# Banded attention and a routed expert layer on one core: the last batch routed in two groups instead of computed densely, ids loaded unchecked, projection writes earlier, score banks by kind

## The reference, cut to what matters

```python
x = _layernorm(x + attention(x))       # 16 heads of 16, key within 64 of the query or before:
                                       # mask = max(causal, window), softmax, out projection
x = _layernorm(x + moe(x))
# moe: 16 experts, top 4 of 16 inside the best 2 of 4 groups, weights normalised, times 2.5
scores = sigmoid(x @ router_weight.T); sc = scores + e_bias
group_scores = sum of the top 2 of each group of 4; keep 2 groups; tidx = top_k(masked, 4)
tw = scores[tidx] / (sum + 1e-20) * 2.5
g = x @ gate_w[e].T; u = x @ up_w[e].T; y = (silu(g) * u) @ down_w[e].T   # 256 -> 128 -> 256
routed = sum over the 4 chosen of tw * y;  shared = the same MLP, width 256, for every token
return routed + shared
```

## Time and profile before

| | us |
|---|---|
| median of 3 runs | 1260.3 (1251.3 to 1264.51) |
| profiled execution | 1256.9, its span 1254.9 |
| PE busy | 1056.3 (84%) |
| DVE busy | 863.1 (69%) |
| ACT busy | 626.5 (50%) |
| POOL busy | 469.5 (37%) |
| granted clock of TensorE, mean | 0.941 |

### The profile page before, as it was taken

One profiled execution on the slowest core, in us unless ns is written; L12 is line 12 of the kernel. 1 busy time (PEld: TensorE's weight loads), 2 busy tenths in 40 slices (PEclk: granted clock), 3 DMA queues, 4 the chain that ended last, 5 costly groups with the idle time before them and its releaser, 6 DMA issues.

```text
span 1254.9 us, 24541 instructions
## 1 busy us (share of the span) xinstructions
PE 1056.3 (84%) x8451; PEld 590.1 (47%) x8451; DVE 863.1 (69%) x1833; ACT 626.5 (50%) x1409; POOL 469.5 (37%) x682
## 2 busy tenths in 40 slices
PE   7696999989777998988997779888898776998895
PEld 4353333344422555544554445454555445654463
DVE  6486787777884666788667676687567556587453
ACT  4323677766444555654555456554455463322332
POOL 7552111152156102223444633214625630286332
PEclk9897999999897999999999899999999898998998
DMA  5753257420123433234366634232636643443320
GB/s 177 214 173 109 69 198 267 125 68 26 49 89 116 62 92 76 58 71 97 98 155 113 169 75 89 61 76 79 150 94 137 181 104 70 136 121 107 90 76 21
DMA packets 181078, 136.07 MB, mean 108 GB/s; under 512 B 105152, under 2 KB 156096, under 8 KB 180960
## 3 DMA queue, kind: packets, MB, share of 16 engines
q1 hardware_dynamic: 170112, 106.17, 33.2%
q0 software_dynamic: 9216, 25.18, 6.4%
q10 hardware_dynamic: 1632, 3.15, 0.9%
HBM read 54.55 MB, written 60.88 MB: 92 GB/s over the span
## 4 chain that ended last, share of the span: by engine, by line
PE 50%; DVE 17%; POOL 12%; issue 11%; ACT 5%; SPq 3%; DMA 2%; DVEq 0%; POOLq 0%; ACTq 0%
PE bank L752 10%; PE bank L575 10%; PE bank L559 8%; PE bank L546 7%; DVE a_mx L1275 5%; POOL a_pool L1076 4%; PE bank L765 3%; PE bank L709 2%; POOL a_QS L1068 2%; POOL rows L1061 2%; ACT a_PT L1137 2%; POOL a_PT L1020 2%; PE bank L659 1%; SPq L838 1%; PE bank L723 1%
## 5 line engine op out<-in xcount | busy, mean ns | idle before, releaser
L1275 DVE TENSOR_REDUCE a_mx<-bank 128x1 f32<-128x512 f32 (+3 forms) x720 | 423.8, 619 | 224.2 <-PE bank L549 144.9
L1137 ACT ACTIVATE a_PT<-bank 128x512 f32<-128x512 f32 (+4 forms) x832 | 374.7, 497 | 224.9 <-PE bank L559 221.3
L559 PE MATMUL bank<-a_QS,a_KS 113*128 113x512 f16 (+4 forms) x832 | 279.8, 344 | 40.3 <-DVE a_mx L1275 32.7
L1020 POOL TENSOR_SCALAR_AFFINE_SELECT a_PT<-a_PT 128x256 f32<-128x256 f32 (+1 forms) x288 | 111.5, 394 | 471.8 <-ACT a_PT L1137 471.1
L546 PE MATMUL bank<-a_KS,a_QS 112*128 112x512 f16 (+4 forms) x832 | 264.6, 340 | 10.4 <-DMA a_KS<-k_dram 5.6
L575 PE MATMUL bank<-a_PT,a_VG 128*17 128x512 f32 (+4 forms) x1664 | 188.3, 527 | 26.6 <-POOL a_PT L1020 26.6
L752 PE MATMUL bank<-e_xt,a_W 128*128 128x128 f16 x1728 | 139.6, 231 | 40.1 <-issue 28.7
L752 PEld LDWEIGHTS bank<-e_xt,a_W 128*128 x1728 | 118.5, 102 | 67.9 <-issue 52.4
L559 PEld LDWEIGHTS bank<-a_QS,a_KS 113*128 113x128 f16 x832 | 82.8, 101 | 121.6 <-DVE a_mx L1275 65.4
L546 PEld LDWEIGHTS bank<-a_KS,a_QS 112*128 112x128 f16 x832 | 81.2, 100 | 103.0 <-ACT a_PT L1137 64.5
L1223 ACT ACTIVATE e_tq<-bank 128x256 f32<-128x256 f32 x96 | 36.8, 383 | 173.1 <-PE bank L752 172.9
(11 more groups left out here) (176 smaller groups left out, 1476.8 us busy)
## 6 DMA issues: line engine op xcount, KB each, us to landing
outs<-e_ys SPq DMA_DIRECT2D x72, 256.0 KB, 2.9
rows<-a_pool SPq DMA_DIRECT2D x48, 256.0 KB, 3.2
a_QS<-c_dram SPq DMA_DIRECT2D x32, 256.0 KB, 3.3
q_dram<-p_qk SPq DMA_DIRECT2D x32, 128.0 KB, 2.1
k_dram<-p_qk SPq DMA_DIRECT2D x32, 128.0 KB, 2.3
v_dram<-p_vs SPq DMA_DIRECT2D x8, 512.0 KB, 3.6
a_QS<-q_dram SPq DMA_DIRECT2D x64, 64.0 KB
a_KS<-k_dram SPq DMA_DIRECT2D x64, 64.0 KB
```

Of the source, the lines that this page charges most:

```text
L559: pe.matmul(ps[:, 0:(qc + 1) * CH - q0], KS[p][0:MR + 1, kt // NT, h % 2, kt % NT * P:kt % NT * P + P], QS[p][0:MR + 1, qc, h, q0 - qc * C ...
L1020: pool.affine_select(out=a, in_=a, compare_op=ALU.is_ge, fill=0.0, base=q0 - (kt * P - WIN), pattern=[[0, 2], [1, w]], channel_multiplier= ...
L1137: act.activation(PT[(G + i) % 2][:, h, 0:w], bank("ST", G, i, h)[:, 0:w], ACT.Exp)\
L1275: dve.tensor_reduce(mx[:, piece, t // NT, heads[0]:heads[0] + n, t % NT], bank("S", G, u)[:, 0:n * w].rearrange("p (h k) -> p h k", h=n), ...
```

## The change

1. Batch 3 is routed like the others, as two groups of one chunk each (`GROUPS`): 32 units, 16 pairs each, with 16 scatters and 16 gathers each. Its chunks get `row_hi` and `row_lo`. The dense code is gone. `slot`, `expert` and `wk` have three buffers. The plan puts behind the attention: group 3's choice at steps 7 to 11, `pos` at 12, its scatters from 16; chunk 7's choice at 22 to 26, `pos` at 27, scatters from 31; the gathers of batch 2 from 42 to 62, behind the last scatter, and their combines in DVE's list at steps 47 to 66; the routed pairs of group 3 from PE's step 43 to 81, of group 4 from 75 to 114; gathers of group 3 from 87, of group 4 from 120.
2. Behind the attention `y` comes 7 steps after `gu` instead of 5, all jobs share seven banks, and rows are loaded 10 steps ahead into eight buffers that lie in the place of the exponentials.
3. Ids are loaded without the check of their bounds.
4. SP writes chunks 2, 3 and 4 before the stacks of round 0.
5. Plain and transposed scores have rings of their own: three and three banks in rounds 0 to 3 (everything else then has bank 7), three and two in the mixed rounds.

The jobs of PE before step 0 stand where they stood.

```diff
-UNITS_B = TOPK * S // P + NE
-NPR = UNITS_B // 2
-NPS = NSH * NT
+GROUPS = [(b, 0, BT) for b in range(B - 1)] + [(B - 1, half * NT, NT) for half in range(NH2)]
+UNITS_OF = [TOPK * n + NE for _, _, n in GROUPS]
+NPS = [n // 2 * NSH for _, _, n in GROUPS]
+NPR = [u // 2 for u in UNITS_OF]
...
+def chunk_of(g, tile):
+    b, j0, _ = GROUPS[g]
+    return b * NH2 + (j0 + tile) // NT
...
+    for g, (b, j0, tiles_) in enumerate(GROUPS):
+        late = b == B - 1
+        for c in sorted({chunk_of(g, t) for t in range(tiles_)}):
+            e = span * (b + 1) + ((3 if late else 6) if c % NH2 else -9)
...
+            ready[c], at = chain(c, e, 0 if c == NC - 2 else 1)
+        gap = 1 if late else 2
+        for n in range(RPARTS):
+            dve[at + 2 + gap * n].append(("route", g, n))
+        q = put(("pos", g), at + gap * RPARTS + 2)
+        for n in range(4):
+            dve[q + 1 + n].append(("place", g, n))
+        for t in range(tiles_):
             for k in range(TOPK):
+                pool[q + 4 + (t * TOPK + k) * 2 // 3].append(("scatter", g, t, k))
+        routed[g] = q + 4 + tiles_ * TOPK * 2 // 3
...
+            sp[q - (5 if q < tail + 10 else 10)].append(("load_rows", g, n))
+            last[g] = y = put(("y", g, n), q + (5 if q < tail else 7))
...
+        at = max(last[g] + 6, w)
+        if g == B - 2:
+            at = max(at, routed[NGR - 1] + 1)
+        for t in range(GROUPS[g][2]):
             for k in range(TOPK):
+                pool[at + (t * TOPK + k) * 2 // 3].append(("gather", g, t, k))
             w = at + (t * TOPK + TOPK) * 2 // 3 + 3
+            dve[w].append(("combine", g, t))
...
-    h, downs = ready[NC - 2] + 1, []
-    for c in (NC - 2, NC - 1):
-        for n in range(NX):
...
+    late_tiles = [a[:].rearrange("p h t -> p (h t)").bitcast(F16)[:, i * 4 * 2 * P:(i + 1) * 4 * 2 * P]
+                  .rearrange("p (k t) -> p k t", k=4) for a in PT for i in range(NXL // 2)]
...
-    RINGS = {"scores": [0, 1, 2, 3, 4], "other": [5, 7], "project": [5, 6, 7], "gates": [0, 1], "ups": [2, 3],
-             "sum0": [4], "sum1": [6]}
+    RINGS = {"s_first": [0, 1, 2], "st_first": [3, 4, 5], "first": [7], "s_rest": [0, 1, 2], "st_rest": [3, 4], "other": [5, 7], "project": [5, 6, 7], "gates": [0, 1], "ups": [2, 3],
+             "end": [5, 7, 0, 1, 2, 3, 4]}
...
-                ps = take("scores", "S", G, u)
+                ps = take("s_first" if round_of[0] < NG else "s_rest", "S", G, u)
...
-                ps = take("scores", "ST", G, i, h)
+                ps = take("st_first" if G < NG else "st_rest", "ST", G, i, h)
...
-                    expert[b % 2][0:1, n:n + REGS], engines=[mybir.EngineType.PE], min_val=0, max_val=NE - 1)
+                    expert[b % 3][0:1, n:n + REGS], engines=[mybir.EngineType.PE], min_val=0, max_val=NE - 1,
+                    skip_runtime_bounds_check_because="the ids are counts of experts that are held to at most NE - 1")
...
-                ring = "other"
+                ring = "first" if h < 2 * NG * NSL else "other" if h < 2 * ATT else "end"
...
+            for c in range(2, 5):
+                project(c)
             for p in range(2):
                 sp.wait_ge(qk_written[p], 128)
                 sp.wait_ge(v_written[p], 16)
...
-            for c in range(2, NC - 1):
+            for c in range(5, NC - 1):
                 project(c)
```

More of the change, by code:

```diff
@@ L186, in plan @@
[L186 to L198, removed]
@@ L200, in plan @@
-    wanted, order = [], {}
[L201 to L219, removed]
+                pool[q + 4 + (t * TOPK + k) * 2 // 3].append(("scatter", g, t, k))
@@ new lines, in plan @@
+        routed[g] = q + 4 + tiles_ * TOPK * 2 // 3
+    wanted, order = [], {}
+    for g in range(NGR):
+        for n in range(NPS[g]):
+            c, tile = shared_place(g, n)
+            wanted.append((ready[c] + tile * 5, g, n))
+        lo = routed[g] + 5
+        hi = routed[g + 1] - 7 if g + 2 < NGR and g < B - 2 else tail if g == B - 2 else lo
+        wanted += [(lo + (hi - lo) * n // NPR[g], g, NPS[g] + n) for n in range(NPR[g])]
+    q, last, second, gu_at = -1, {}, [], []
+    for h, g, n in sorted(wanted):
+        order[g, n] = len(order)
+        q = put(("gu", g, n), max([h, q + 1] + [y + 1 for y in second[1 - NHB:2 - NHB]]))
+        gu_at.append(q)
+        act[q].append(("tanh", g, n))
+        dve[q + 1].append(("gate", g, n))
+        act[q + 2].append(("hh", g, n))
+        dve[q + 3].append(("hl", g, n))
+        if n >= NPS[g]:
+            sp[q - (5 if q < tail + 10 else 10)].append(("load_rows", g, n))
+            last[g] = y = put(("y", g, n), q + (5 if q < tail else 7))
@@ L240, in plan @@
                 sp[w + 5].append(("store", c))
-    h, downs = ready[NC - 2] + 1, []
-    for c in (NC - 2, NC - 1):
-        for n in range(NX):
[L245 to L257, removed]
     end = 1 + max(max(a) for a in (pe, act, dve, pool, sp))
-    return pe, act, dve, pool, sp, end, order
+    return pe, act, dve, pool, sp, end, order, gu_at
 RPARTS = 5
-PE_AT, ACT_AT, DVE_AT, POOL_AT, SP_AT, END, ORDER = plan()
+PE_AT, ACT_AT, DVE_AT, POOL_AT, SP_AT, END, ORDER, GU_AT = plan()
 PAIRS = list(ORDER)
+NXT, NXL = 3, 8
+ROUTED = [q for q, (g, n) in enumerate(PAIRS) if n >= NPS[g]]
+LATE = next(i for i, q in enumerate(ROUTED) if GU_AT[q] >= 2 * ATT + 10)
 class Waits:
@@ L685, in fill @@
                     ps = take(ring, "pos", b)
[L686 to L689 removed]
+                    i0, n = mask_at(b), GROUPS[b][2]
+                    m = M[:, i0:i0 + n + 1].rearrange("p t e -> p (t e)")
+                    pe.matmul(ps[:, 0:(n + 1) * NE], before[:], m, start=True, stop=True)
```

416 lines of the change are left out of this document (140 added, 276 removed).

## The result

The changed kernel takes **1216.84 us** (median of 4 runs, 1215.25 to 1220.68), the kernel before 1260.91 beside it (4 runs): ratio 0.9664, 95% interval 0.9615 to 0.9714. The forecast was 1214 in a range of 1188 to 1246. The sum was right and most of its parts were not: the unchecked ids gave nearly all of it, and the routed end, which is most of the diff, next to nothing.

What follows compares the result with a forecast made beforehand. PE sets the pace, with holes; POOL decides the routed end. Early writes 9, ids 18 and 5, banks 2, end 11 sum to 45, giving 1212 or 1215; forecast 1214 us, range 1188 to 1246.

Steps and rivals of the forecast that it cites:

- Early writes: At the start, SP writing chunks 2 to 4 first removes PE's 12 us stall; gain 9 us, bounds 5 and 12.
- V and the writes of chunk 5 move behind the stacks: At the start, these later SP jobs fall under a stretch that DVE's maxima bound, so they cost nothing.
- Ids: Mainly in the mixed rounds, unchecked loads remove PE idle time, 18 us (bounds 6 and 28), plus 5 us of clock.
- Half the holes' clock drops would go: Behind id loads, half of 12 us of half-clock stretches vanishes: 5 us, bounds 0 to 12.
- Rival D: At the id loads, the check is hidden: PE meets DVE's maxima, 6 of 23 us are left; 1231, chance 0.11.
- rival B: DVE's order doesn't hold PE in the end (17 more), or ids give 10 more; 1197 to 1204, chance 0.17.
- Banks: In the rounds, splitting plain and transposed score banks moves the wait, which hardly shrinks; gain 2 us, bounds -12 and +12.
- Rival A: In the mixed rounds, two transposed-score banks make PE wait for ACT, 0.4 us a slot, 62 us; 1276, chance 0.08.
- The end: Behind the mixed rounds, routing the last batch with POOL deciding ends at 1244; gain 11 us, bounds -10 and +28.
- what is left there: In the routed end behind step 72, PE's remaining gate/up steps, down steps and id loads take 51 us.
- Rival C: The end runs at half clock, short groups alternating with waits, which adds 26 us; 1240, chance 0.12.
- a sign for being wrong: In the routed end, PE idling over 20 us in all between its first and last routed pair shows the prediction wrong.

Runs made afterwards that it cites:

- experiment 2: Kernel before, with only the projections of chunks 2 to 4 written ahead of the first stack; 1256.46 us, ratio 0.9953.
- experiment 3: Kernel before, with only the score banks split (three and three, then three and two); 1262.72 us, ratio 1.0021.
- experiment 6: Changed kernel, with five shared banks for the score matmuls among the projections; 1215.98 us, ratio 0.9626 to the kernel before.
- experiment 1: Kernel before, with only the ids loaded unchecked; 1220.59 us, ratio 0.9672.
- experiment 11: Kernel before, with ids still checked but loaded four at a time instead of eight; 1247.53 us, ratio 0.9869.
- experiment 8: Changed kernel, with the last batch's expert weights at constant addresses instead of by loaded ids; 1215.64 us, ratio 0.9594 to the kernel before.
- experiment 4: Kernel before, with unchecked ids, early writes and split banks together, the last batch still dense; 1218.19 us, ratio 0.9664.
- experiment 5: Changed kernel, with combines of batch 2 and group 3 later in DVE's order and batch 2's gathers spread; 1201.91 us, ratio 0.9502 to the kernel before.
- experiment 7: Changed kernel, with later combines of batch 2 and group 3 and five banks among the projections; 1196.17 us, ratio 0.949 to the kernel before.
- experiment 10: Changed kernel, with later combines, five banks among the projections, and batch 1's last two combines three steps later; 1191.76 us, ratio 0.9434 to the kernel before.
- experiment 9: Changed kernel, with all scores on five shared banks again (split undone); 1219.15 us, ratio 0.9637 to the kernel before.

## Why the prediction was right, and which steps were not

**Sum.** Forecast 45 off, measured 40.3 between the two profiled executions and 44 between the medians. The ids gave 12 more than forecast, the mixed rounds of the one trace 4 beside that where the banks were to give 2, the early writes fell short by 9 and the end by about 10. That these misses cancel to within 5 us is luck.

**Early writes (9, measured 0 where it counts).** The queue went as worked out: nine issues, no stall of 12 us, a wait for the stack in its place. The wait was 7.1 and not 5, as chunk 4's writes ended at 57.8 and not 55. The first score matmul came 5.8 us earlier, and at the start of the rounds nothing of it was left. The failed step is "V and the writes of chunk 5 move behind the stacks, under a stretch that DVE bounds (maxima), so nothing" together with the banks part, which priced three banks in the first rounds as "a pure gain" and did not look at the projections, where scores had five and got three. Experiments 2, 3 and 6 show it: 4.8 us earlier alone, 4.0 later with the split alone, 5.7 earlier with only the projections' banks given back.

**Ids (18 and 5, measured 21 and 14).** The mechanism, the place and the sign were right. The mis-sized term is the clock: "Half the holes' clock drops would go" gave 5, experiment 1 measured 14 (9 to 18 against the other kernels with checked ids), so more than 5 is shown, more than the bound of 12 is not. Of the 28 us of holes 21 came back, 75% and not 65; the transposed scores waited for DVE about as long as before (29.7 against 32.7 us). Rival D, the check hidden, is refuted. The second half of rival B, 10 more from the ids, came true, without its time. Experiment 11 adds that the hole's length matters more than the number of checks.

**Banks (2, bounds -12 and 12, measured -2 to 1).** "The wait moves, it hardly shrinks" is what experiment 3 shows, 32.6 of 32.7 us; what it gave in the mixed rounds it took at the start. Rival A had its place right and its price wrong: transposed scores waited for ACT 8.2 us in 12 waits, 0.05 us a slot and not 0.4.

**The end (11, measured 1.4).** Counted from the end of the rounds, POOL's chain came as worked out:

| from the last round's end | predicted | measured |
|---|---|---|
| first scatter | 28.4 | 27.6 |
| last scatter | 71.4 | 73.7 |
| PE's last long hold ends | 123.4 | 123.8 |
| PE's last matmul | 179.4 | 192.2 |
| end of the program | 221.4 | 230.9 |

The failed step is "what is left there: 17 gate/up steps x 1.92, 22 down steps x 0.65 and four id loads, 51 us": with the 5 for group 3's combines 56, and 68.4 measured. The last long hold was at step 68, four steps ahead of the one named, so 20 pairs and 23 down steps were left; a pair took 2.15 us; and 7.2 of the 68.4 us were idle. The row for 1.92 is a single pair; in a row of pairs the queue itself is the pace. The end chain gave 3 us back (38.7 instead of 42). The Trainium skill's figure of 55.6 ns per 128 columns ("TensorE: Matmul & The Clock Gate", section "Wait — 56ns, not 53.3ns?") was set aside for the row. It gives 1.33 us a pair, and experiment 8 measured 1.34 once the weights stood at constant addresses: the figure and the row were both right, of different things.

By the gains alone the end was worth less still. Experiment 4's dense end took 229.0 us and the changed kernel's 230.9 and 229.9: with all else equal, routing the last batch moved nothing that can be measured, and the 1.4 can be put down to the unchecked ids (experiment 1 won 3.1 behind the rounds with the dense end). The prediction named a sign for being wrong here, more than 20 us of PE idle in the routed end, and it came: 26.8 us. It had priced the last hold, and taken as done ahead of it three pairs that the order kept behind it. Experiments 5 and 7 show what is to be had when DVE's order doesn't hold PE: 12 and 18 us in this stage, one execution each.

**Rival C** (half clock in the end) was partly true: 0.77 for 60 us, where 0.52 throughout was priced. By the Trainium skill's same page, section "HAM oscillation — how this bites in real kernels", thin tiles with waits between them run throttled again and again. The trace agrees for the stretch with the holds; experiment 5's 1.00 with the same tiles says that here the waits count and not the tiles. Its next stretch, with holds of at most 1.6 us, had 0.90.

**What stays open.** Why round 15 takes 59 us in some executions and 62 to 66 in others (the changed kernel twice, and experiments 7 and 10, against experiments 1, 4, 5, 6, 8 and 9) was not settled; the hold it comes from is that of a down step behind batch 1's combine. How much clock the checks cost is known to within 9 to 18 us only, and whether shorter holes save any of it is open.

## What to carry to other kernels

A check in the queue of the engine that sets the pace costs twice: as idle time, and again as a lower clock behind it; take it away, or cut it into pieces that the queue's lead covers. In an order written by hand, a job that waits for a transfer belongs so late that the transfer has landed when the engine comes to it, since all that other engines wait for stands behind it: moving twelve combines, and spreading the gathers before them, was worth 15 us where replacing 155 us of dense work had been worth one at most. And a gain in one stage is read at the next border: the early writes' 6 us were gone 35 us later, spent on banks.

## What the runs showed of the hardware

- A matmul of 128 columns whose weight address comes from a register costs 90 ns in a row of such (2.15 us for 24), 56 ns with a constant address (1.34 us), though the register operation is only 46 ns long and stands ahead of two in three. Behind score matmuls of 512 columns it costs nothing: a pair in the mixed rounds took 1.34 us as well.
- The price of reading ids into registers goes nearly with their number: 594 ns for eight, 332 ns for four.
- Sixteen loads of checked ids, which PE saw as holes of 1.3 to 3 us, took 9 to 18 us in lower clock on top of 21 us of idle time. The same 144 checks in twice as many loads, with holes of at most 1.6 us, took 15 us less of the whole.
